# Moving the third decay tile of a slot behind the first output part in a hand-ordered Mamba-2 layer

## The reference, cut to what matters

```python
proj = hidden_states @ in_proj_w.T            # gate, x, B, C, dt
hBC  = silu(conv1d(hBC, conv_w) + conv_b)     # four taps over time
Lmat = exp(segment_sum(Ac))                   # decay between positions of a chunk
M    = Gm * Lmat                              # Gm = C B^T
Y_diag = einsum('bclsh,bcshp->bclhp', M, xch)
y = (Y_diag + Y_off) + D * x
y = y * rsqrt(mean(y*y)) * norm_w * silu(gate)
return y @ out_proj_w.T
```

## Time and profile before

| what | value |
|---|---|
| median of three runs | 2432.32 us (2431.52 to 2433.32) |
| the profiled execution's own time | 2436.1 us |
| span of that execution, first to last instruction | 2434.3 us |
| PE busy, share of the span | 2236.8 us, 92% |
| DVE busy | 1642.8 us, 67% |
| ACT busy | 1175.1 us, 48% |
| POOL busy | 686.7 us, 28% |
| mean granted TensorE clock | 0.963 |

### The profile page before, as it was taken

One profiled execution on the slowest core, in us unless ns is written; L12 is line 12 of the kernel. 1 busy time (PEld: TensorE's weight loads), 2 busy tenths in 40 slices (PEclk: granted clock), 3 DMA queues, 4 the chain that ended last, 5 costly groups with the idle time before them and its releaser, 6 DMA issues.

```text
span 2434.3 us, 34263 instructions
## 1 busy us (share of the span) xinstructions
PE 2236.8 (92%) x13940; PEld 1740.2 (71%) x13940; DVE 1642.8 (67%) x1707; ACT 1175.1 (48%) x1747; POOL 686.7 (28%) x318
## 2 busy tenths in 40 slices
PE   4589999999999999999999999994799889999987
PEld 2478877777777777787887777773378657777754
DVE  5667767777777776777776777675822347777754
ACT  2244545445545554454454545451533247777741
POOL 1023343334333333343334333422344200000000
PEclk8789999999999999999999999997999989999998
DMA  1111011101011010111101110100122110000000
GB/s 66 47 37 37 28 45 37 36 28 54 28 37 37 29 51 30 37 38 44 37 28 44 38 36 28 45 19 4 31 80 95 59 27 16 21 22 22 10 24 35
DMA packets 41627, 89.31 MB, mean 37 GB/s; under 512 B 13824, under 2 KB 22912, under 8 KB 41088
## 3 DMA queue, kind: packets, MB, share of 16 engines
q1 hardware_dynamic: 41472, 87.12, 11.5%
HBM read 83.82 MB, written 3.28 MB: 36 GB/s over the span
## 4 chain that ended last, share of the span: by engine, by line
PE 67%; DVE 15%; ACT 5%; issue 4%; DMA 4%; POOL 3%; SPq 0%; ACTq 0%; DVEq 0%
PE PS L472 15%; PE PS L473 14%; PE PS L474 14%; DVE arena L1220 5%; DMA arena<-in_w_xg 4%; PE PS L703 3%; PE PS L550 3%; PE PS L788 3%; POOL wol L393 2%; PE PS L773 2%; PE PS L466 2%; DVE arena L1250 1%; ACT arena L907 1%; PE PS L795 1%; PE PS L762 1%
## 5 line engine op out<-in xcount | busy, mean ns | idle before, releaser
L472 PE MATMUL PS<-xnh,wh 128*128 128x512 f32 x1272 | 512.4, 403 | 23.4 <-DVE xnl L1160 10.9
L474 PE MATMUL PS<-xnh,wl 128*128 128x512 f32 x1272 | 499.3, 393 | 0.0
L473 PE MATMUL PS<-xnl,wh 128*128 128x512 f32 x1272 | 498.9, 392 | 0.0
L1220 DVE SCALAR_TENSOR_TENSOR arena<-PS,arena 128x1020 f32<-128x1020 f32 (+2 forms) x240 | 305.5, 1273 | 93.1 <-ACT arena L920 47.3
L385 POOL TENSOR_TENSOR arena<-arena 128x1024 f32<-128x1024 f32 x64 | 173.2, 2706 | 464.4 <-ACT arena L899 464.4
L472 PEld LDWEIGHTS PS<-xnh,wh 128*128 128x128 f32 x1272 | 240.4, 189 | 83.4 <-issue 20.7
L474 PEld LDWEIGHTS PS<-xnh,wl 128*128 128x128 f32 x1272 | 240.4, 189 | 51.1
L473 PEld LDWEIGHTS PS<-xnl,wh 128*128 128x128 f32 x1272 | 240.7, 189 | 46.5
L380 POOL TENSOR_TENSOR wl<-arena,wh 128x1024 fp32r<-128x1024 f32 x72 | 172.6, 2397 | 301.2 <-ACT wh L882 301.2
L887 ACT ACTIVATE PS<-PS 128x1024 f32<-128x1024 f32 x128 | 129.2, 1009 | 264.9 <-PE PS L519 264.9
L472 PE MATMUL PS<-zh,woh 128*128 128x512 f32 x512 | 215.0, 420 | 26.2 <-DVE arena L1220 16.9
(11 more groups left out here) (221 smaller groups left out, 4274.5 us busy)
## 6 DMA issues: line engine op xcount, KB each, us to landing
arena<-in_w_xg SPq DMA_DIRECT2D x72, 512.0 KB, 3.7
arena<-in_w_o SPq DMA_DIRECT2D x32, 512.0 KB, 3.6
arena<-in_w_f SPq DMA_DIRECT2D x28, 512.0 KB, 3.5
arena<-in_w_h SPq DMA_DIRECT2D x16, 257.0 KB
arena<-scr SPq DMA_DIRECT2D x256, 6.0 KB
x<-in_x SPq DMA_DIRECT2D x1, 2048.0 KB, 7.6
arena<-scr SPq DMA_DIRECT2D x128, 3.0 KB
out<-x SPq DMA_DIRECT2D x1, 2048.0 KB, 6.3
```

The lines of the kernel that those rows point to most:

```text
L472: mm(PS[:, bank], ah, bh, start=(n == 0), stop=False)
L473: mm(PS[:, bank], ah, bl, start=False, stop=False)
L474: last = mm(PS[:, bank], al, bh, start=False, stop=(n == len(terms) - 1))
L1220: ins = stt(o, pair_of(bank).rearrange("p q (b t) -> p q b t", t=SEQ)[:, :, :, :SEQ - k], w[:, 3 - k:4 - k], o, ALU.mult, ALU.add)
```

## The change

On TensorE, in all slots with output parts, the eight matmuls of decay tile 2 stand between the first and the second output part instead of ahead of both. On VectorE the weighing of tile 2 stands behind the sum of the first output part; in slots 4 and 5 silu_bc is thereby ahead of both. Nothing is added and nothing left out. ScalarE's, GpSimd's and SP's orders are as before; exp_of and rows wait for tile 2 wherever it stands.

```diff
@@ TensorE, group @@
                         wide(GB, (o + 1) % 2, 1).then_inc(s["g_ps"], 1)
-                    falls(t, k, 2)
+                    if not outs:
+                        falls(t, k, 2)
                     if outs:
                         q = PPG * g + i // 2 - 1
                         if n is not None:
...
                         pe.wait_ge(s["wolo"], q + 1)
                         pe.wait_ge(s["zlo"], 2 * q + 3)
                         out_part(2 * k, XB)
+                        falls(t, k, 2)
                         if n is not None:
                             pe.wait_ge(s["sgd"], t + 2)
@@ VectorE, group @@
                         silu_x(n, 1 - k)
-                    weigh(t, 2)
                     if side in (0, 1):
                         silu_bc(g + 1, side)
                     if not (first and i < 2):
                         out_sum(2 * k, XB, 2 * t - 3)
+                    weigh(t, 2)
+                    if not (first and i < 2):
                         out_sum(2 * k + 1, GB, 2 * t - 2)
```

## The result

The changed kernel takes 2463.5 us (median of four runs, 2461.5 to 2467.2) against 2432.8; the ratio is 1.0128 with an interval of 1.0111 to 1.0146. The forecast was 2462.8, range 2446 to 2478. The profiled execution is the slowest of its four: 2467.2 us, 31.1 above the profiled one of before.

What follows compares the result with a forecast made beforehand. The prediction took TensorE's own work as the bound, busy 1427 of 1470 us. Its terms, 15.7 + 10.3 + 1.6 - 2.0 + 4.9 = 30.5 us, added to 2432.3 gave 2462.8 us, range 2446 to 2478.

Steps and rivals of the forecast that it cites:

- The mechanism: On TensorE the third tap sets the first output part's start; moving tile 2 only takes work out of that wait.
- The 29 slots: Slots where the output part waited for the third tap: tile 2 now paid in full, 0.54 us each, 15.7 us.
- The 25 slots: Odd-kind slots without a visible wait: TensorE gains 0.13 us and pays 0.54, +0.41 each, 10.3 us.
- Slot 4: Slot 4 of seven groups, VectorE's order: `outputs` 1.0 us later, most given back, +0.23 each, 1.6 us.
- The last slot: The first output part runs in tile 2's 3.40 us wait: 2.0 us gained, bounds 0 and 3.4.
- The queues: SP's rows and weight transfers and ScalarE's rounding come about 3 us later but stay hidden: costs nothing.
- The clock: The unbroken wait brings three more falls of the granted clock behind the 15 long waits: 4.9 us, bounds 0 and 9.7.
- the cheap tile: Rival: the tile between the output parts costs only the lower bounds, 12.8 us more in all, 2445 us; chance 0.13.
- the free tile: Rival: the tile's matmuls run free beside their neighbours between the output parts, sum -3.7 us, 2428.6 us; chance 0.05.
- VectorE as the bound: Rival: the weighing behind a sum ends after the second output part in all slots, 2479 us; chance 0.07.
- the late weight: Rival: the weight transfer behind rows misses its use in 15 even slots, 1 us each, 2478 us; chance 0.02.
- the clock that stays up: Rival: with tile 2 later the nine falls of the clock disappear, 14.6 us less than today, 2443 us; chance 0.05.

Runs made afterwards that it cites:

- e1: TensorE's half of the change alone, VectorE's old order kept, against the kernel before: 2485.7 us, ratio 1.0203.
- e5: The changed kernel with the third tap ahead of the weighing of tile 1 on VectorE: 2415.0 us, ratio 0.9913.
- e2: VectorE's half of the change alone, tile 2 still ahead of both output parts, against the kernel before: 2440.3 us, ratio 1.0028.
- e9: The changed kernel with tile 2 at its old place in even slots and the new one in odd slots: 2451.5 us, ratio 1.0073.
- e3: The changed kernel with tile 2's eight matmuls done at the old place as well: 2479.2 us, ratio 1.0180.
- e8: The kernel before with silu_bc ahead of the weighing of tile 2 in slots 4 and 5: 2428.5 us, ratio 0.9976.
- e6: The kernel before with the third tap ahead of the weighing of tile 1, tile 2 at its old place: 2467.4 us, ratio 1.0132.
- e4: The changed kernel with tile 2's eight matmuls done twice in a row at the new place: 2477.8 us, ratio 1.0177.
- e7: e5 with the weighing of tile 2 ahead of both sums, behind silu_bc, in slots 4 and 5: 2399.7 us, ratio 0.9853.

## Why the prediction was right

**The mechanism held as written:** the output part starts when the third tap allows, and the tile is no longer in that wait. e1 shows that TensorE's half does it, and e5 that the third tap is the thing waited for: with the tap 1.13 us earlier the wait is about 1 us shorter, or gone.

**The 29 slots.** Priced at 0.54 us, 15.7 in all, with 4.9 for the clock: 20.6. The trace has 13.5 + 4.2 + 4.5 = 22.2. The tile costs 0.59 to 0.60 (6.28 against 5.69 in slot 24; 24.76 against 24.17 in slot 5). The 0.05 above the forecast is in the next ten steps behind the tile, which are mostly 0.23 to 0.24 us instead of 0.227.

**The 25 slots.** 0.41 each against 0.43 measured. That the tile hid a wait there of which the trace of before showed nothing was read from the end of the third tap in the earlier trace rows, and the new waits (61 instead of 29) confirm it.

**Slot 4.** 0.23 against 0.32. `outputs` starts 1.1 us later (forecast 1.0), and 0.7 coming back was right; e2 has the same 28.2 us, so this growth is VectorE's order alone. silu_bc is 1.22 us there, as the term needed. Slot 5 was taken as covered, and is (no wait of `outputs` there after the change), but e2 shows that the cover is the tile's own delay, and e5, where the output parts start earlier, that it is thin: 0.7 us of wait in slot 5.

**The last slot.** From the start of tile 1 to `outputs` it took 11.54 us and takes 9.42: 2.1 against 2.0. What stands behind `outputs` takes 1.1 us more in the profiled execution, within what it varies by in the traces (773.7 to 776.9 us), so 1.0 is left of it there.

```profile
1676.50 0.61 PE L519 MATMUL PS<-arena 6*128 6x128 bf16 x8 [1.42 <-DVE arena L1252]
...
1682.46 0.58 PE L519 MATMUL PS<-arena 6*128 6x128 bf16 x8
...
1685.92 0.44 PE L550 MATMUL PS<-arena 128*64 128x128 f32 x4
```

**The queues.** Nothing, as priced. The delay was read too small: in slot 24 the tile moves from 1.17 us ahead of the first output part to 2.97 behind its start, 4.1 us and not 3.1. The weight transfer is issued 5.3 us behind the start of the first output part instead of 1.2. Its user still starts 7.1 us after that, 2.6 more than the transfer's 4.5:

```profile
729.57 0.36 SPq L288 DMA_DIRECT2D arena<-in_w_xg  x1
...
736.68 1.05 ACT L884 ACTIVATE wh<-arena 128x1024 fp32r<-128x1024 f32 x1
```

**The clock: the number was right by luck, and its reason is not shown.** Three more falls were forecast, and the profiled execution has 12 instead of nine. I gave the unbroken wait as the reason. With the broken wait there are 14 falls in e9, 11 in e2, 10 in e3 and six in e8; with the unbroken wait 15 in e1, 14 in e6, 11 in the second trace of the changed kernel and 10 in e4. Each is the count of one execution. The two groups overlap, so the form of the wait does not fix the count. What the runs do show is that no fall follows a short wait: in e5 and e7 there is one fall each, and it stands behind slot 34, the one wait that is still long (2.7 and 2.9 us), and none behind the other 14 of 1.2 to 1.6 us. In e5:

```profile
947.67 0.50 PE L472 MATMUL PS<-zh,woh 128*128 128x512 f32 x1 [2.73 <-DVE arena L1222]
```

That the total came within 1 us of the measured is partly chance: in the profiled execution the terms of the stage sum to 35.3 us, and 3.2 of them are offset ahead of the stage. The clock's term of 4.9 rests on a count that differs by several falls between kernels with the same waits.

The rivals: the cheap tile and the free tile fall with the 0.59 us of slot 24, VectorE as the bound with the waits of `outputs` (7 times, 0.6 us), the late weight with the rows above, and the clock that stays up with 12 and 11 falls in the two traces of the changed kernel.

## What to carry to other kernels

Ask of each small piece of work on the busiest engine which wait it stands in: where that wait ends does not depend on the piece, a piece inside it is free, and the same piece behind it is paid for: here 0.6 us in the 29 slots that waited, and 0.4 in the 25 where the piece just covered the wait. The move pays only together with something that makes the wait shorter: alone it cost 31 us, but with the third tap ahead of the weighing it is worth 52 (e6 against e5), because then nothing on the way to the output part needs that weighing. About 18 of the 52 are falls of the clock (14 and one). And where two engines slow each other, as silu_bc and GpSimd's pass do here, the order on one of them can decide which of them keeps its time.

## What the runs showed of the hardware that I had not expected

- A block of eight matmuls of 6 rows by 128 columns between blocks of 128x512 costs 0.6 us, of which the matmuls are 0.18 (e4); the switch in and out is the rest.
- The granted clock goes to the 1.2 GHz level behind idle stretches of 1.9 to 3.4 us (mostly 2.0 to 2.7) in anything from six (e8) to all 15 (e1) of the places, and the count differs between kernels whose waits are alike: nine before, six in e8, 14 in e9. A fall costs about 1.4 us (24.5 against 25.8 to 26.0 us for the same kind of slot). The mean over the stretch from 310 to 1640 us, the changed kernel and then e5:

```profile
310.00:1640.00 1330.00, 1276.37 (x8544) 1014.98 (x8543) 955.09 (x755) 653.12 (x645) 478.73 (x194) 0.98 0.11 36
```

```profile
310.00:1640.00 1330.00, 1293.96 (x8874) 1040.51 (x8875) 984.92 (x783) 676.39 (x669) 488.91 (x200) 1.00 0.11 37
```

Of the 49 us by which e5 is faster than the changed kernel, 11 falls fewer at 1.4 us are 15. No run here shows what beyond the length of the wait decides on a fall.
